# Mask rows by transfer to VectorE, and ScalarE's down steps ahead of the turned x, in a cross-attention and mixture-of-experts kernel

## The reference

```python
def xattn(hidden, memory, mask):
    scores = einsum('bsd,bmd->bsm', hidden, memory) / sqrt(D)
    scores = where(mask[:, None, :], scores, -1e+30)
    readout = einsum('bsm,bmd->bsd', softmax(scores), memory)
    return where(any(mask, -1)[:, None, None], readout, 0)

def ffn(x, G, gate_w, up_w, down_w, lora_A, lora_B):
    value, indices = top_k(softmax(x @ G), 2)
    w = einsum('bsk,bske->bse', value, one_hot(indices, 8))
    gated = silu(einsum('bsh,efh->bsef', x, gate_w)) * einsum('bsh,efh->bsef', x, up_w)
    out = einsum('bsef,bse,ehf->bsh', gated, w, down_w)
    return out + einsum('bser,bse,ehr->bsh', einsum('bsh,erh->bser', x, lora_A), w, lora_B)

x = x + xattn(layernorm(x), ctx_2048, mask)
x = x + ffn(layernorm(x), ...)
```

## Time and profile before

| | |
|---|---|
| median of three runs | 531.51 us |
| the profiled execution, its span | 529.37 us, 527.6 us |
| TensorE busy, its weight loads | 500.1 us (95%), 437.0 us (83%) |
| VectorE busy | 471.0 us (89%) |
| ScalarE busy | 344.9 us (65%) |
| GpSimd busy | 286.0 us (54%) |
| HBM read and written | 114.04 and 78.73 MB, 365 GB/s over the span |

### The profile page before, as it was taken

How to read it: one execution, slowest core, us unless ns; L and a number is a source line. 1 busy time by engine, 2 the same in 40 slices (tenths; PEclk the granted TensorE clock), 3 DMA queues, 4 the chain that set the end, 5 groups by cost and what they waited for, 6 DMA issues and landing times.

```text
span 527.6 us, 16394 instructions
## 1 busy us (share of the span) xinstructions
PE 500.1 (95%) x4040; PEld 437.0 (83%) x4040; DVE 471.0 (89%) x1921; ACT 344.9 (65%) x927; POOL 286.0 (54%) x397
## 2 busy tenths in 40 slices
PE   8999999999999999697899999999999999999994
PEld 7888888888888777586779799988999999989982
DVE  5999999999999987578888899988999999999885
ACT  4787888777888787467667778777544444444441
POOL 4237677677777677644444344444454544545444
PEclk9999999999999999899999999999999999999997
DMA  8999999999999989999997999967999999999832
GB/s 309 401 342 338 395 403 367 412 395 386 407 398 389 398 278 317 384 367 383 350 346 271 359 394 369 367 230 271 418 413 417 416 416 415 417 414 415 360 133 79
DMA packets 65609, 189.12 MB, mean 358 GB/s; under 512 B 9582, under 2 KB 9710, under 8 KB 65520
## 3 DMA queue, kind: packets, MB, share of 16 engines
q1 hardware_dynamic: 44352, 120.20, 61.1%
q0 software_dynamic: 20800, 67.65, 32.5%
q10 hardware_dynamic: 368, 0.22, 0.2%
HBM read 114.04 MB, written 78.73 MB: 365 GB/s over the span
## 4 chain that ended last, share of the span: by engine, by line
PE 66%; DVE 13%; issue 12%; ACT 6%; DMA 1%; another core or an unknown queue 1%; POOL 1%; POOLq 0%; ACTq 0%; DVEq 0%
PE bank L516 11%; PE rd L516 10%; PE bank L494 9%; PE bank L367 6%; PE rd L532 6%; PE rd L533 5%; PE rd L407 4%; PE bank L346 3%; PE rd L408 3%; PE rd L380 3%; PE rd L523 2%; DVE z_shared L1128 2%; ACT xn L602 2%; DVE ggT_b L1118 1%; DVE ggT_a L1117 1%
## 5 line engine op out<-in xcount | busy, mean ns | idle before, releaser
L671 ACT COPY hT<-bank 128x512 f32<-128x512 f32 x140 | 81.8, 585 | 55.4 <-PE bank L494 50.3
L516 PE MATMUL bank<-wg_sb,hT 128*128 x560 | 81.4, 289 | 0.4 <-issue 0.4
L516 PE MATMUL rd<-wg_sb,hT 128*128 x560 | 80.2, 286 | 0.0
L367 PE MATMUL bank<-cc_sb,xnT 128*128 128x136 f32 x512 | 80.1, 286 | 0.0
L1238 POOL DMA_INDIRECT x_rows<-xe x64 | 65.2, 1019 | 23.4 <-issue 19.8
L516 PEld LDWEIGHTS bank<-wg_sb,hT 128*128 128x128 f32 x560 | 73.5, 192 | 0.9 <-issue 0.9
L516 PEld LDWEIGHTS rd<-wg_sb,hT 128*128 128x128 f32 x560 | 72.7, 190 | 0.1
L532 PE MATMUL rd<-dn_a,ggT_a 128*128 x140 | 67.3, 481 | 4.8 <-DVE ggT_b L1118 2.9
L367 PEld LDWEIGHTS bank<-cc_sb,xnT 128*128 128x128 f32 x512 | 68.3, 191 | 1.0
L1253 POOL DMA_INDIRECT out_x<-z_shared x41 | 39.8, 972 | 42.6 <-issue 35.2
L1128 DVE SCALAR_TENSOR_TENSOR z_shared<-rd,z_shared 128x512 f32<-128x512 f32 x77 | 57.6, 748 | 1.9 <-PE rd L533 0.2
(11 more groups left out here) (167 smaller groups left out, 1182.2 us busy)
## 6 DMA issues: line engine op xcount, KB each, us to landing
cc_sb<-in_cc SPq DMA_DIRECT2D x64, 532.0 KB
z_shared<-z_rows SPq DMA_DIRECT2D x41, 516.0 KB
x_sb<-in_x SPq DMA_DIRECT2D x64, 256.0 KB
z_own<-z_rows SPq DMA_DIRECT2D x29, 516.0 KB
z_shared<-x_rows SPq DMA_DIRECT2D x36, 260.0 KB
z_own<-x_rows SPq DMA_DIRECT2D x34, 260.0 KB
z_rows<-pad SPq DMA_DIRECT2D x8, 516.0 KB
wg_sb<-in_wg SPq DMA_DIRECT2D x8, 288.0 KB
```

Source lines behind the costliest of these rows:

```text
L367: mm = pe.matmul(sc_ps[:, 0:S + E], xnT[:, n % 2, k, :], by_feature(n, k, S + E), start=False, stop=(k == KD - 1))
L516: mm = pe.matmul(gu_ps[q % 2][:, 0:GU], hT[:, q % 2, k, :], wg_flat[:, bass.ds(at + k * GU, GU)], start=(k == 0), stop=(k == KD - 1))
L671: act.copy(hT[:, q % 2, :, :], hT_ps[q % 2][:].rearrange("p (k s) -> p k s", k=KD)).then_inc(hT_ready, 1)
```

## The change

It has three parts.

1. For tiles 16 to 63 the bias product leaves TensorE. SyncE writes `bias` to memory once (at n = 7), and reads it back in six transfers, each for eight tiles, with the same 2 KB for all 128 partitions (at n = 12, 20, 27, 36, 44, 51, for tiles 16, 24, 32, 40, 48, 56). They go to buffers that the second half uses (`z_own`, `hT`). VectorE's masking op adds these bfloat16 rows in place of the zeros; in the first tile of each eight it waits for the transfer.
2. On ScalarE, `down_hi` and the second step stand ahead of `keep_xT`, and the second step comes one iteration later than before, in the iteration of the sum.
3. For odd i only the 32 rows that differ from those of i - 1 are loaded (64 KB). `down_hi` treats these 32 rows, and the other 96 are copied from `dn_a` of step i - 1, once that step's sum is done (`down_same`, in place of `down_left`).

```diff
+MR = 8
+SPREAD_AT = {2: 12, 3: 20, 4: 27, 5: 36, 6: 44, 7: 51}
...
+        def spread(i):
+            rows = hT[:].rearrange("p j k s -> p (j k s)") if i >= 6 else z_own[:, (i - 2) // 2, :]
+            at = i % 2 * (MR * S // 2)
+            return rows[:, at:at + MR * S // 2].bitcast(BF16)
...
             for n in range(5, B):
+                if n == 7:
+                    sp.wait_ge(bias_ready, 2)
+                    sp.dma_start(mask_rows[:], bias[0:B, 0:S]).then_inc(mask_kept, 16)
+                for i in [i for i, at in SPREAD_AT.items() if at == n]:
+                    sp.wait_ge(mask_kept, 16)
+                    sp.dma_start(spread(i), bass.AP(tensor=mask_rows.tensor, offset=i * MR * S, ap=[[0, P], [1, MR * S]])).then_inc(mask_spread[i], 16)
...
-                    sp.dma_start(dn_part(i).bitcast(F32), dn[:, i % 2, i // 2, :]).then_inc(dn_loaded, 16)
+                    if i % 2 == 0:
+                        sp.dma_start(dn_part(i).bitcast(F32), dn[:, i // 2, :]).then_inc(dn_loaded, 16)
+                    else:
+                        sp.dma_start(dn_part(i)[KG:P, :].bitcast(F32), dn_rest[:, i // 2, :]).then_inc(dn_loaded, 16)
...
+            sp.wait_ge(masked_ready, 6 * MR)
             for q in range(2 * NQ):
...
+                if n < 2 * MR:
+                    pe.matmul(sc_ps[:, 0:S + E], tile_of[:, n:n + 1].broadcast_to([P, S]), bias[:], start=True, stop=False)
...
+            def down_same(i):
+                act.wait_ge(dn_ready, i)
+                act.copy(dn_part(i)[0:KG, :], dn_part(i - 1)[0:KG, :].bitcast(F32)).then_inc(dn_low_left, 1)
...
+                if t + 2 in SUMS_AT:
+                    down_hi(SUMS_AT.index(t + 2))
+                if t in SUMS_AT:
+                    i = SUMS_AT.index(t)
+                    if i % 2 == 0:
+                        down_left(i)
+                    else:
+                        down_same(i)
                 if in_sweep(t, 0):
                     keep_xT(t)
...
-                if t + 2 in SUMS_AT:
-                    down_hi(SUMS_AT.index(t + 2))
-                if t + 1 in SUMS_AT:
-                    down_left(SUMS_AT.index(t + 1))
...
+                i, b = divmod(n, MR)
+                if i >= 2 and b == 0:
+                    dve.wait_ge(mask_spread[i], 16)
+                hidden = zeros[:] if i < 2 else spread(i)[:, b * S:(b + 1) * S]
+                dve.tensor_tensor_reduce(masked[:, n % 2, :], sc_ps[:, 0:S], hidden, -SCALE, 3e38, ALU.add, ALU.min,
...
             def down_parts(i):
                 pool.wait_ge(dn_low_left, i + 1)
+                pool.wait_ge(dn_hi_ready, i + 1)
...
+            pool.memset(dn_hi[:, 1, :], 0.0).then_inc(dn_hi_set, 1)
```

More of the change, by code:

```diff
@@ L93, with xattn_moe @@
 NCONST = PACK + len(GROUPS)
-def xattn_moe(nc, x, cc, mask, wg, dn, g, consts, out):
+def xattn_moe(nc, x, cc, mask, wg, dn, dn_rest, g, consts, out):
     with ExitStack() as stack:
@@ L179, in rows_of @@
             return z_own[:, slot, :] if slot < RO else z_shared[:, slot - RO, :]
+        mask_rows = nc.dram_tensor("mask_rows", (B, S), BF16).ap()
         x1_rows = nc.dram_tensor("x1_rows", (ROWS, XW), F32).ap()
@@ L188, in xattn_moe @@
             sem, ("const_loaded", "g_loaded", "wg_loaded", "dn_loaded", "dn_hi_ready", "dn_low_left", "dn_ready"))
-        mask_loaded = sem("mask_loaded")
+        mask_loaded, mask_kept = sem("mask_loaded"), sem("mask_kept")
+        mask_spread = {i: sem(f"mask_spread{i}") for i in SPREAD_AT}
         set_up, ones_set, pad_set, before_ready = sem("set_up"), sem("ones_set"), sem("pad_set"), sem("before_ready")
@@ L200, in xattn_moe @@
             sem, ("strips_done", "strips_ready", "prod_done", "prod_ready", "part_ready"))
-        after_set = sem("after_set")
+        after_set, dn_hi_set = sem("after_set"), sem("dn_hi_set")
         top_ready, which_ready, pair_ready, gap_step, turn_step, lexp_ready, hot_ready = map(
@@ L215, in xattn_moe, with down_rows @@
                   "again", "y_done", "z_ready"))
+        def spread(i):
+            rows = hT[:].rearrange("p j k s -> p (j k s)") if i >= 6 else z_own[:, (i - 2) // 2, :]
+            at = i % 2 * (MR * S // 2)
+            return rows[:, at:at + MR * S // 2].bitcast(BF16)
         def dn_part(i):
             return (dn_a, dn_b)[i % 2][:, i // 2, 0:D]
+        def down_rows(i):
+            return slice(0, P) if i % 2 == 0 else slice(KG, P)
         def left(q, ring):
@@ L362, in scores @@
                     pe.wait_ge(before_ready, 1)
-                pe.matmul(sc_ps[:, 0:S + E], tile_of[:, n:n + 1].broadcast_to([P, S]), bias[:], start=True, stop=False)
+                if n < 2 * MR:
+                    pe.matmul(sc_ps[:, 0:S + E], tile_of[:, n:n + 1].broadcast_to([P, S]), bias[:], start=True, stop=False)
                 for k in range(KD):
@@ L366, in scores @@
                         turn_prob(n - 1)
-                    mm = pe.matmul(sc_ps[:, 0:S + E], xnT[:, n % 2, k, :], by_feature(n, k, S + E), start=False, stop=(k == KD - 1))
+                    mm = pe.matmul(sc_ps[:, 0:S + E], xnT[:, n % 2, k, :], by_feature(n, k, S + E), start=(n >= 2 * MR and k == 0), stop=(k == KD - 1))
                 mm.then_inc(scores_done, 1)
@@ L609, in down_hi @@
                     act.wait_ge(dn_ready, i - 1)
-                act.activation(dn_hi[:, i % 2, :].bitcast(F32R), dn_part(i).bitcast(F32), ACT.Copy, scale=const_sb[:, SIGN:SIGN + 1]).then_inc(dn_hi_ready, 1)
+                if i == 1:
+                    act.wait_ge(dn_hi_set, 1)
+                own = down_rows(i)
+                act.activation(dn_hi[own, i % 2, :].bitcast(F32R), dn_part(i)[own, :].bitcast(F32), ACT.Copy, scale=const_sb[own, SIGN:SIGN + 1]).then_inc(dn_hi_ready, 1)
+            def down_same(i):
+                act.wait_ge(dn_ready, i)
+                act.copy(dn_part(i)[0:KG, :], dn_part(i - 1)[0:KG, :].bitcast(F32)).then_inc(dn_low_left, 1)
             def down_left(i):
@@ L747, in mask_scores @@
                     dve.wait_ge(prob_ready, n - 1)
-                dve.tensor_tensor_reduce(masked[:, n % 2, :], sc_ps[:, 0:S], zeros[:], -SCALE, 3e38, ALU.add, ALU.min,
+                i, b = divmod(n, MR)
[3 more added lines that the diff above has]
+                dve.tensor_tensor_reduce(masked[:, n % 2, :], sc_ps[:, 0:S], hidden, -SCALE, 3e38, ALU.add, ALU.min,
                                          rowmin[:, n % 2, :]).then_inc(masked_ready, 1)
@@ L1306 @@
     down, lora_b = down.transpose(2, 0, 1), lora_b.transpose(2, 0, 1)
-    back = np.stack([np.concatenate([down[:Q], lora_b, lora_b, down[Q:], again], 0) for again in (down[:Q], down[Q:])], 1)
+    back = np.concatenate([down[:Q], lora_b, lora_b, down[Q:], down[:Q]], 0)
     consts = np.zeros((P, NCONST), np.float32)
@@ L1327 @@
         consts[j * GP:j * GP + E, at:at + E] = np.eye(E)
-    arrays = {"x": x, "cc": cc, "mask": mask, "wg": into, "dn": back, "g": g, "consts": consts}
+    arrays = {"x": x, "cc": cc, "mask": mask, "wg": into, "dn": back, "dn_rest": down[Q:], "g": g, "consts": consts}
     arrays = {f"in_{n}": np.ascontiguousarray(a) for n, a in arrays.items()}
```

## The result

The changed kernel took 535.3 us in the median of 20 runs (533.1 to 540.8), the kernel before 532.9 beside it (20 runs): a ratio of 1.0057, 95% interval 1.0037 to 1.0077. The ratios come from repeated runs outside a chip's slower state, which took one run in all (of d_apart_2), and aren't quotients of the medians, which here would be 1.0045. On two other chips of the experiments, where the kernel before takes 513 us instead of 532, the same kernel stood at 1.0159 and 1.0163. The first profile of before is from a chip of the 532 us kind.

A forecast was written before the change was run, and what follows sets the result against it. The prediction took VectorE, TensorE and the DMA engines as full together in the sweep. The stalls' +1.85 us less the middle's 1.0 gave +0.85, so 532.3 us on the three runs' scale, range 529.8 to 535.2.

The forecast's parts named there:

- The transfers: Six mask transfers in the sweep: x-load rate, 0.66 us each; 400 KB extra early make x tiles up to 1.0 us later.
- The forecast for the middle: Tiles 8 to 56, ScalarE's steps moved: gain 0 to 2.5 us, with the transfers -1.0 to 2.5, taken as 1.0.
- Rival C: Slower by the six transfers: at half the rate 537.5 us, at three quarters of the rate 534.8; chance 0.13.
- The waits of steps 13 and 15: Iterations 56 to 63: ScalarE's copies wait for GpSimd's sum; tile 59's scores 1.25 us late, sweep ends 1.85 us later.
- rival D: Slower by the clock: stalls leave TensorE idle some 2 us each, a lower-clock stretch costs 1.7 us, 534.0; chance 0.20.
- ScalarE's order: Steps ahead of the copy of the turned x: TensorE's 5.4 us of waits go, VectorE's share inside 2.5 us.
- My wait at step 13: Iteration 59: ScalarE, done with pT at some 192.4 us, stands until GpSimd's sum ends at 195.0.
- the start of the expert blocks: After the sweep: hangs on the last readouts and an activation that waits 4.64 us, neither touched, so as before.
- The bias product: Tiles 16 to 63: 48 matmuls go, 2.9 us of TensorE; before 190 us it counts only by removing VectorE's waits.
- the operand: VectorE's masking op with bfloat16 rows for float32 zeros, 48 tiles: at most 3.2 us either way, taken as 0.
- rival B: Faster, no stall or a sooner sum: last iterations -1.6 us, of it 1.2 for pT; 527.4 or 528.9; chance 0.13.
- The scale: Whole kernel: three runs' median 531.51 us, 2.1 above the profiled execution's 529.37, so the forecast reads 532.3.

The follow-up runs named there:

- d_apart_2: The changed kernel with the six transfers reading 128 different rows of zeros (mask left out from tile 16), third chip: 518.4 us, 1.0102.
- b_prod: The changed kernel without the mask transfers, bias product on TensorE for all 64 tiles, both ScalarE waits kept, first chip: 531.6 us, 0.9989.
- c_none: The changed kernel without mask transfers and without the bias product from tile 16 (mask left out), first chip: 529.9 us, 0.9973.
- after: The profiled run of the changed kernel beside the result: 538.97 us, where the median of 20 runs is 535.3.
- d_apart: The changed kernel with the six transfers reading 128 different rows of zeros (mask left out from tile 16), first chip: 532.0 us, 0.9999.
- after_3: The changed kernel again, unedited, on the third chip (before 513.5 us): 521.4 us, 1.0163.
- before_2: The kernel before, unchanged, profiled again on the fourth chip, where it takes 513.8 us.
- l_own13: The changed kernel without transfers, product in all tiles, only step 13 loading its own whole rows, fifth chip: 511.8 us, 0.9963.
- l_own15: The changed kernel without transfers, product in all tiles, only step 15 loading its own whole rows, fifth chip: 515.2 us, 1.0036.
- b_prod_2: The changed kernel without transfers, product in all tiles, waits at steps 13 and 15 kept, fourth chip: 517.1 us, 1.0047.
- a_own: The changed kernel with steps 13 and 15 loading all their own 128 rows, so without their waits, first chip: 535.0 us, 1.0071.
- f_order: The kernel before with only ScalarE's two down-row steps moved ahead of its copy of the turned x, second chip: 511.5 us, 0.9963.
- g_prod_own: The changed kernel without transfers, product in all tiles, steps 13 and 15 loading whole rows, second chip: 510.1 us, 0.9934.
- a_own_2: The changed kernel with steps 13 and 15 loading all their own 128 rows, so without their waits, third chip: 513.6 us, 1.0006.
- g_prod_own_2: The changed kernel without transfers, product in all tiles, steps 13 and 15 loading whole rows, fourth chip: 510.3 us, 0.992.
- after_2: The changed kernel again, unedited, on the second chip (before 513.3 us): 520.4 us, 1.0159.
- i_shared: The changed kernel with all 128 partitions reading one 2 KB piece of input zeros (mask left out), third chip: 521.6 us, 1.0156.

## Why the prediction was wrong, by its steps

**The transfers: the step that failed for the first chip.** I took a read of one 2 KB piece at the rate of the x loads, and so no more than 1.0 us for all six. The forecast for the middle was a gain of 1.0 us; tiles 18 to 57 lost 2.7 (126.0 for 123.3), and 2.0 and 3.0 on two 513 us chips. Without transfers they gained: 121.3 in b_prod, 2.0 us, inside my 0 to 2.5. With the bytes read apart it is 122.9, to be set against c_none's 121.0, which has no product either. So the extra early bytes cost 1.9 us, about twice my 1.0, and the repeated source 3.1 more (126.0 less 122.9). These are single profiles, and the standstills without a named cause lie in these stretches too: after has two, of 1.0 and 1.1 us, d_apart two, of 0.7 and 1.1, b_prod, c_none and before none. So on this chip part of both terms may be theirs, and no run parts them; the 513 us chips, which have none, lost as much in the middle with the transfers. The runs say the same: 0.9999 to 1.0057 is 3.1 us, and 1.0102 to 1.0163 on the third chip as well, though there the intervals overlap. The longer packets explain somewhat under half of that by themselves: 48 packets on each engine, 29 ns longer (119 less 90), are 1.4 us; the rest was not followed.

Rival C had the mechanism, and the packets were at its three quarters of the rate (89 of 119 ns is 0.75). That its time of 534.8 us lies near the 535.3 measured is luck: it gave the transfers 1.4 us, where the runs show 3.6, and the waits 1.85, where taking them away saved nothing here, and it stands on a median of before that was 1.4 us lower.

**The waits of steps 13 and 15: the chain held, its price did not on the 513 us chips.** Counted from the masking of tile 57, the maskings of tiles 59, 61 and 63 come 1.1, 1.1 and 2.0 us later in after than in before, where I had 1.25, 1.0 and 1.85 (the first and the last for the scores). In after_3 against before_2 they come 2.2, 2.5 and 3.4 us later. So the first delay is carried to the last tile, as in the prediction's chain, and on these chips it is larger by what the clock costs, a term that I had left out of the sum and put in rival D: 1.85 + 1.6 is 3.45, and 3.4 to 3.6 were measured against before. (The expectations of l_own13 and l_own15 give the forecast the view that the last wait alone decides. The prediction adds 1.25 us of the first, 1.0 by tile 61, and 0.85 of the second.) Against a kernel without the waits they cost 6.5 to 6.8 us, since ScalarE's order alone would have saved 1.4 us in these tiles, and b_prod_2 was at half clock for 6.8 us, twice as long as after_3.

My wait at step 13 was 2.6 us; 3.1 and 3.7 were measured. GpSimd is not why: its sum ends 5.6 us after the masking of tile 57, and 5.5 and 5.4 us in before and before_2. ScalarE comes to the copy sooner than the 2.9 us after that masking that I had, at 2.5 and 2.0.

On the first chip taking the waits away saved nothing, and I had said that the start of the expert blocks would be untouched: from tile 63 to th, 7.5 us stood in place of 10.8, since the wait of 4.64 us is not in after. In a_own the 29.4 us from tile 57 to th stayed as in after, with three stretches at half clock between 204 and 246 us and two new standstills, of ScalarE and of VectorE:

```profile
204.05 0.27 ACT L616 COPY g_parts<-rd 128x128 f32<-128x128 f32 x1 [2.09 <-remote]
...
204.18 0.29 DVE L793 CUSTOM_DVE_ANT_0 masked<-bank,hT 128x128 f32<-128x128 f32 x1 [2.62 <-remote]
```

What causes them is open: the profile names no engine of this core. All six profiles from the 532 us kind have such standstills of 0.9 us or more, and none of the fourteen from 513 us chips.

**Rival D** held on the 513 us chips, in place and price (1.7 us; measured 1.6). On the 532 us kind it held in two of four profiles with the wait. In after TensorE stood here, and the clock stayed at 1.00:

```profile
203.24 0.73 PE L393 MATMUL bank<-cc_sb,xnT 128*128 128x136 f32 x4 [2.08 <-ACT xnT L601]
```

c_none is like it. b_prod and d_apart stood as long (2.0 and 2.1 us), were then at half clock for 3.4 us, and took 23.4 and 23.1 us from tile 57 to 63 where those two took 21.9: 1.2 to 1.5 us more. What tells the two pairs apart is open. Between the first 18 us and 500 us after's only stretch at half clock came at 229.6, as one came at 221.3 in before; so that one was not new.

**The bias product and the operand.** 48 products were 2.9 us of TensorE's time by my sum, and 0.9 to 1.7 us of the kernel's at most. The operand costs nothing, as taken (289 and 288 ns). No masking op of after waited for a transfer, as taken too.

**ScalarE's order.** Its gain is real, 1.9 us by itself on a 513 us chip, and 1.4 of it lie in the last tiles, where rival B had put 1.2 us for the vanished waits for pT. The middle gained only together with the smaller loads, if at all: 120.8 to 122.3 us in five profiles without transfers, for 122.5.

**The scale.** I set the sum on the median of three runs of before, 531.5; twenty runs beside the changed kernel gave 532.9. So 1.4 of the 3.0 us between my 532.3 and the 535.3 measured are not the change's, and against before it took 2.4 us more in the medians (3.0 by the ratio), where I had 0.85. And I took one profile as the kernel. Its expert blocks take 307.4 us and those of before_2 297.0, and the difference starts where VectorE waits for ScalarE's th. The stretch at the blocks' start in before:

```profile
DVE t L1101 <- ACT th L677: 11.1, 8, 4.3
```

and in before_2, same stretch (218 to 262 us):

```profile
DVE t L1101 <- ACT th L677: 0.5, 1, 0.5
```

The ledger for a 513 us chip, each term a difference of ratios times 513: order -1.9 us (f_order); six smaller loads -1.5 (g_prod_own against f_order); transfers less what the product's removal gives +3.7 (a_own_2 against g_prod_own; +4.4 against g_prod_own_2); waits +6.5 (b_prod_2 against g_prod_own_2). The sum is +6.8 (+7.5 with the other transfer term), and the whole change stood 8.2 and 8.4 us above before by its ratios, 7.1 and 7.9 by the medians. The terms come from several chips, and each is uncertain by 1 to 2 us (that of the loads by nearly its size), so the ledger closes only within that. The version to keep is g_prod_own: the order, six small loads, whole loads for steps 13 and 15, the product left on TensorE. It beat before by 3.2 and 3.5 us on the 513 us chips; on the first it was not run.

## What to carry to other kernels

Price a new wait by what stands idle behind it on every engine, and on TensorE add a stretch at half clock (1.6 us here) if the wait leaves it empty for as long as 2 us; let waits on a chain add up unless a row shows the slack that absorbs them. Where the DMA share is 1.0, moving work from an engine to a transfer moves it to the resource that has no room. Before trusting a sum made from one profile, look for what is particular to that run: a standstill that nothing in the kernel makes can hide or swallow the very term you are pricing.

## What the runs showed of the hardware

- Reading one 2 KB piece of memory into 128 partitions makes packets of 107 to 126 ns on average (after, a_own, after_2, after_3, a_own_2, i_shared), where 128 different pieces take 86 to 90 (d_apart_2, d_apart). Sixteen copies changed nothing (121 and 123 ns).
- One chip ran the kernel before in 532.3 us, four others in 513.3 to 513.8. From 50 to 180 us the sweep moves 396 GB/s in before and 400 in before_2; what differs is the expert blocks. From 260 to 300 us, before and then before_2:

```profile
260.00:300.00 40.00, 37.25 (x263) 32.79 (x262) 35.27 (x124) 28.44 (x70) 16.37 (x17) 1.00 0.90 325
```

```profile
260.00:300.00 40.00, 39.61 (x290) 35.99 (x291) 36.87 (x129) 30.55 (x74) 17.67 (x19) 1.00 1.03 409
```

- TensorE empty for 2.0 to 2.1 us at iteration 59 left the clock at 1.00 in two profiles (after, c_none) and was followed by 3.4 us at half clock in two (b_prod, d_apart). In all eight profiles with 2.64 or 2.65 us such a stretch came, of 3.4 us in seven, of 6.8 in b_prod_2.
- Standstills of ScalarE or VectorE of 0.9 us or more that no engine of the core ends: in all six profiles from the 532 us kind of chip (0.9 to 4.6 us), in none of fourteen from the 513 us kind.
